# A graph-attention kernel on one core: how the sorted table is turned and decoded between its two edge loops

## What is computed

```
# layer 0
f    = (edge_attr @ fc_w.T).reshape(-1, 4, 128)
feat = sum_over_heads(leaky_relu(attn[edge_type] * f, 0.2))
x    = layernorm(x + segment_sum(x[src] + feat, dst))
# layer 1, on the new x; softmax over the edges of one src
h    = x @ W.T + b;  s1 = h @ a1 + a1b;  s2 = h @ a2 + a2b
e    = leaky_relu(s1[src] + s2[dst], 0.01)
att  = softmax of e over each src
x    = layernorm(x + segment_sum(att * h[dst], src))
```

## Time and profile before

| | |
|---|---|
| median of three runs | 2538.67 us |
| the profiled execution | 2536.95 us, its span 2535.1 us |
| busy share of the span | TensorE 86%, VectorE 91%, ScalarE 77%, GpSimd (POOL) 72% |
| first loop, stage between, second loop | until about 1497 us, 1497 to 1548 us, from 1548 us |

### The profile page before, as it was taken

How to read it: one execution, slowest core, us unless ns; L and a number is a source line. 1 busy time by engine, 2 the same in 40 slices (tenths; PEclk the granted TensorE clock), 3 DMA queues, 4 the chain that set the end, 5 groups by cost and what they waited for, 6 DMA issues and landing times. The chain is left out here.

```text
span 2535.1 us, 49366 instructions
## 1 busy us (share of the span) xinstructions
PE 2173.4 (86%) x12265; PEld 1562.1 (62%) x12266; DVE 2299.6 (91%) x5975; ACT 1950.8 (77%) x5574; POOL 1824.8 (72%) x1746
## 2 busy tenths in 40 slices
PE   6999999999999999999999974766667777777674
PEld 3566666666666666666666654766667666776664
DVE  9999999999999999999999986778887778888886
ACT  5788888888888888888888854777777777776666
POOL 3477777777777777777777745777777777776662
PEclk8999999999999999999999986899998888888886
DMA  4233333333333333333333324444444444443332
GB/s 139 73 101 104 104 106 101 104 103 104 105 106 102 103 103 104 105 106 101 104 102 105 105 58 98 99 100 100 98 101 99 99 100 101 98 99 86 84 82 71
DMA packets 180816, 250.92 MB, mean 99 GB/s; under 512 B 41103, under 2 KB 110172, under 8 KB 180416
## 3 DMA queue, kind: packets, MB, share of 16 engines
q1 hardware_dynamic: 125088, 145.72, 20.2%
q0 software_dynamic: 55456, 102.13, 17.1%
HBM read 238.37 MB, written 9.31 MB: 98 GB/s over the span
## 5 line engine op out<-in xcount | busy, mean ns | idle before, releaser
L627 POOL DMA_INDIRECT room<-in_x,pk x784 | 925.2, 1180 | 262.5 <-issue 252.5
L1010 PE MATMUL FP<-fc_sb,room 128*128 128x512 f32 x1568 | 832.4, 612 | 2.2 <-issue 2.2
L1019 PE MATMUL WP<-at_p,rel_oh 100*128 100x512 f32 x1568 | 804.2, 594 | 0.0
L671 POOL DMA_INDIRECT room<-h_rows,y x666 | 628.9, 944 | 220.5 <-issue 184.9
L754 ACT ACTIVATE w_sb<-WP 128x512 f32<-128x512 f32 x784 | 464.1, 592 | 224.9 <-PE WP L1019 219.5
L1019 PEld LDWEIGHTS WP<-at_p,rel_oh 100*128 100x128 f32 x1568 | 297.9, 190 | 376.4 <-issue 376.4
L1108 PE MATMUL FP<-ident,room 128*128 128x128 f32 x1664 | 278.2, 319 | 277.3 <-DMA room<-h_rows,y 213.9
L1359 DVE TENSOR_TENSOR z<-FP,w_sb 128x1024 f32<-128x1024 f32 x392 | 478.8, 1221 | 1.5 <-ACT w_sb L754 1.0
L1366 DVE SCALAR_TENSOR_TENSOR y<-z 128x2048 f32<-128x2048 f32 x196 | 452.2, 2307 | 0.0
L1108 PEld LDWEIGHTS FP<-ident,room 128*128 128x128 f32 x1664 | 238.0, 220 | 312.9 <-DMA room<-h_rows,y 246.0
L1010 PEld LDWEIGHTS FP<-fc_sb,room 128*128 128x128 f32 x1568 | 266.6, 190 | 43.3 <-issue 2.6
(11 more groups left out here) (280 smaller groups left out, 3475.5 us busy)
## 6 DMA issues: line engine op xcount, KB each, us to landing
room<-in_e SPq DMA_DIRECT2D x196, 256.0 KB
rel_sb<-in_rel_g SPq DMA_DIRECT2D x196, 200.0 KB
z<-sorted_sources SPq DMA_DIRECT2D x208, 128.0 KB
room<-in_x,pk POOLq DMA_INDIRECT x784
room<-h_rows,y POOLq DMA_INDIRECT x666
w_sb<-far_rows SPq DMA_DIRECT2D x100, 65.0 KB
w_sb<-near_records SPq DMA_DIRECT2D x101, 61.0 KB
sorted_edges<-runs,spot_i POOLq DMA_INDIRECT x196, 2.0
```

The costliest lines, as they stand in the source:

```text
L627: pool.indirect_dma_start(xg[:, k, u, 0:P], None, x[:, :], bass.IndirectOffsetOnAxis(ap=pk[:, g, u:u + 1], axis=0)).then_inc(xg_in[k], 16)
L671: pool.indirect_dma_start(hg[k][:, u, :], None, h_dram[:, :], bass.IndirectOffsetOnAxis(ap=sd[:, g * TG + u:g * TG + u + 1], axis=0)).then ...
L1010: mm = pe.matmul(FP[u // 2][:, u % 2, :], e_sb[:, k, u, :], fc_sb[:, :], start=True, stop=True)
L1019: mm = pe.matmul(WP[u % 2][:, :], rel_oh[:, k % 2, u * P:(u + 1) * P], at_p[:, j, :], start=(j == 0), stop=(j == 1))
```

## The change

1. TensorE no longer waits for the sum of the sides. It waits for the table itself and adds the sides in PSUM: for each of the eight tiles two matmuls against the identity, one per side.
2. VectorE's sum, casts and mask of the table leave the pass for chunk 4 and stand behind the last chunk, after the shift L1490.
3. SP's two stores of them stand behind its last store of h.
4. ScalarE's queue stores the last ten rows of the last four blocks, in place of POOL's (the count moves from `h_small` to `h_out`).
5. POOL reads the number of further groups ahead of its h stores, in place of behind them. It waits for `s_loc` ahead of the gathers of group 4, whose buffer is the memory of `tab_sum`.

```diff
@@ sync
-                if c == HCHUNKS // 2:
-                    sp.wait_ge(s_loc, 1)
-                    sp.dma_start(loc_dram..., loc_b...).then_inc(loc_out, 16)
-                    sp.dma_start(near_dram..., loc_i[NEAR_PER * TG - 1:P:NEAR_PER * TG, :]...).then_inc(near_out, 16)
+            sp.wait_ge(s_loc, 1)
+            sp.dma_start(loc_dram..., loc_b...).then_inc(loc_out, 16)
+            sp.dma_start(near_dram..., loc_i[NEAR_PER * TG - 1:P:NEAR_PER * TG, :]...).then_inc(near_out, 16)
             sp.wait_ge(loc_out, 16)
             sp.wait_ge(near_out, 16)
@@ gpsimd
             pool.memset(o_all, 0.0).then_inc(o_zero, 1)
-            for c in range(HCHUNKS):
+            more = group_count(pool)
+            for c in range(HCHUNKS - 1):
                 pool.wait_ge(n_hb, HC * (c + 1))
                 pool.dma_start(h_blocks[PMAIN:BN, HC * c:HC * (c + 1), :],
                                h_sb[PMAIN:BN, HC * c:HC * (c + 1), 0:HROW]).then_inc(h_small, 16)
-            pool.wait_ge(h_out, 16 * HCHUNKS)
-            pool.wait_ge(h_small, 16 * HCHUNKS)
+            pool.wait_ge(h_out, 16 * (HCHUNKS + 1))
+            pool.wait_ge(h_small, 16 * (HCHUNKS - 1))
...
-            more = group_count(pool)
             for k in range(S1):
+                if k == SLOTS:
+                    pool.wait_ge(s_loc, 1)
                 group1(k, k, True)
@@ scalar
-
+            act.wait_ge(n_hb, NS)
+            act.dma_start(h_blocks[PMAIN:BN, NS - HC:NS, :], h_sb[PMAIN:BN, NS - HC:NS, 0:HROW]).then_inc(h_out, 16)
             act.wait_ge(s_dec, 1)
@@ tensor
                 if c == HCHUNKS // 2 - 2:
-                    pe.wait_ge(t_sum, 1)
+                    pe.wait_ge(s_srt, 32)
                     for u in range(CH):
-                        mm = pe.transpose((EPS_T, AP_)[u // 4][:, u % 4 * P:(u % 4 + 1) * P],
-                                          tab_sum[:, u * P:(u + 1) * P], ident[:, :])
+                        for side_of in range(2):
+                            mm = pe.matmul((EPS_T, AP_)[u // 4][:, u % 4 * P:(u % 4 + 1) * P],
+                                           tab[:, side_of, u * P:(u + 1) * P], ident[:, :],
+                                           start=(side_of == 0), stop=(side_of == 1))
                     mm.then_inc(t_turned, 1)
@@ vector
-                if c == HCHUNKS // 2 - 2:
-                    dve.wait_ge(s_srt, 32)
-                    v.tensor_tensor(tab_sum, tab[:, 0, :], tab[:, 1, :], ALU.add).then_inc(t_sum, 1)
-                    dve.wait_ge(t_sum, 1)
-                    link(v.tensor_copy(loc_i, tab_sum))
-                    link(v.tensor_scalar(loc_m, loc_i, 255, P - 1, ALU.bitwise_and, ALU.bitwise_xor))
-                    v.tensor_copy(loc_b, loc_m).then_inc(s_loc, 1)
             dve.wait_ge(t_cast, 1)
             v.tensor_scalar(sd, both, 8, None, ALU.arith_shift_right).then_inc(s_dec, 1)
+            dve.wait_ge(s_srt, 32)
+            v.tensor_tensor(tab_sum, tab[:, 0, :], tab[:, 1, :], ALU.add).then_inc(t_sum, 1)
+            dve.wait_ge(t_sum, 1)
+            link(v.tensor_copy(loc_i, tab_sum))
+            link(v.tensor_scalar(loc_m, loc_i, 255, P - 1, ALU.bitwise_and, ALU.bitwise_xor))
+            v.tensor_copy(loc_b, loc_m).then_inc(s_loc, 1)
             link(v.tensor_scalar(ss, both, 255, P - 1, ALU.bitwise_and, ALU.bitwise_xor))
             dve.wait_ge(s_loc, 1)
             dve.wait_ge(near_out, 16)
             v.tensor_copy(ssf, ss).then_inc(s_ssf, 1)
```

More of the change, by code:

```diff
@@ L544, in _ @@
                              h_sb[0:PMAIN, HC * c:HC * (c + 1), 0:HROW]).then_inc(h_out, 16)
-                if c == HCHUNKS // 2:
-                    sp.wait_ge(s_loc, 1)
[L547 to L550, removed]
+            sp.wait_ge(s_loc, 1)
+            sp.dma_start(loc_dram.rearrange("g (u r) -> (g u) r", r=P).rearrange("(c p) r -> p c r", p=P),
+                         loc_b.rearrange("p (c r) -> p c r", r=P)).then_inc(loc_out, 16)
+            sp.dma_start(near_dram.rearrange("(c a) r -> a c r", c=CH),
+                         loc_i[NEAR_PER * TG - 1:P:NEAR_PER * TG, :].rearrange("p (c r) -> p c r", r=P)).then_inc(near_out, 16)
             sp.wait_ge(loc_out, 16)
@@ L595, in _ @@
             sp.sem_inc(sp_turn, 1)
-            sp.wait_ge(h_out, 16 * HCHUNKS)
-            sp.wait_ge(h_small, 16 * HCHUNKS)
+            sp.wait_ge(h_out, 16 * (HCHUNKS + 1))
+            sp.wait_ge(h_small, 16 * (HCHUNKS - 1))
             for q0, q1 in CHUNKS:
```

## The result

Twenty runs of the changed kernel have a median of 2542.64 us (2540.93 to 2545.30), twenty of the one before 2537.90 us (2536.13 to 2540.43). The ratio is 1.0019, with a 95% interval of 1.0013 to 1.0025: slower by 4.7 us, between 3.3 and 6.3. The forecast was +4.7 us and 2543.4 us, with a hole in the stream of gathers that GpSimd (POOL) issues as its cause.

What follows compares the result with a forecast made beforehand. POOL's gather stream was taken to bound loop 2. VectorE 5.2 us late (+5.9 from L1490 to the cast, less 0.6), less 0.5 of gap, gives +4.7: 2538.67 + 4.7 = 2543.4 us, range 2539.3 to 2546.0.

Steps and rivals of the forecast that it cites:

- The bound: Loop 2: POOL's gathers, about 1.25 us each, have no slack for about 750 us, so any delay moves everything behind.
- Part 1, chunk 5: Pass for chunk 4: TensorE's table matmuls replace VectorE's decode, so chunk 5's statistics begin 0.6 us earlier, not 3.3.
- Part 2, the near store: Behind the last chunk: VectorE's cast into `ssf` waits for the near store, landing 2.6 us after issue; preparation 5.2 us late.
- Part 3, POOL: Start of POOL's stream: first gather some 3.2 us earlier, then 8 us idle for ScalarE's copy; short loop's gather +4.7 us.
- L690 0.3 us after it: POOL's short-loop gather L690 goes 0.3 us, the gap of its stream, after ScalarE's copy L908 ends: at 1556.25.
- a span that grows less than L690 moved: Sign of a wrong forecast: total time grows less than the short loop's gather shifts, meaning unseen slack in loop 2.
- The first gather decides: Rival at POOL's stream start: group 2 follows the first eight gathers, gaining 3.2 us, 2535.5 us; chance 0.08.
- Matmuls at half clock: Rival at TensorE's table matmuls: all run at half clock, 3.8 + 0.6 us more, +9.1, 2547.8 us; chance 0.05.
- The near store lands late: Rival on SP's queue: near store shares the 256 KB store's 3.8 us, 1.2 more; +5.9, 2544.6 us; chance 0.15.
- The delay is taken up later: Rival in loop 2's last 48 steps: consumers are the bound there, loss shrinks to about +1, 2539.7 us; chance 0.12.

Runs made afterwards that it cites:

- two parts and later: Kernel before plus ScalarE's store of the last rows, POOL's early read and the short loop behind group 3's gathers; 2535.67 us beside 2539.16, ratio 0.9987.
- store and read only: Kernel before with only ScalarE's queue storing the last ten rows and POOL reading the group count early; 2537.64 us beside 2538.13, ratio 0.9999.
- own buffer: Changed kernel with the integer sum in other memory, so VectorE's cast to `ssf` skips the near store's wait; 2540.29 us beside 2538.13, ratio 1.0007.
- later, own buffer: Changed kernel with the short loop behind group 3's gathers and the integer sum in its own memory; 2534.02 us beside 2539.16, ratio 0.9979.
- tiles spread: Changed kernel, short loop behind group 3, table matmuls spread over passes for chunks 3 to 10, ScalarE's casts moved to chunk 11; 2531.71 us beside 2539.16, ratio 0.9971.
- short loop later: Changed kernel with POOL running the short loop behind the gathers of group 3, not group 1; 2533.56 us beside 2538.13 before, ratio 0.9979.

## Why the prediction was right, point by point

- **The bound.** That POOL's stream is the bound of loop 2 and passes a shift on is shown: stream shifts of +5.3, -0.2, +0.1, +2.3, -4.7, -2.9, -6.5 and -3.7 us go with medians of +4.7, +0.2, -0.5, +2.2, -4.6, -3.5, -7.4 and -5.1 us, in the order of the table. At the 600th gather of the stage, some 730 us later, the shifts are still +5.5, -0.1, +0.1, +2.7, -4.7, -1.8, -6.6 and -3.8 us; only "two parts and later" lost a microsecond on the way. Behind that, where the last 48 steps have another bound, the shift of the last gather differs from these by up to 1.5 us in single traces.
- **Part 1, chunk 5.** 0.6 us was forecast and 1.1 was measured. The matmuls took 0.11 us each and not 0.125, the rate of loop 2. That it would be far less than 3.3 was right.
- **Part 2, the near store.** Forecast: `s_loc` at 1538.0, cast at 1541.2, 5.2 us late. Measured: the decode ends at 1536.76 + 0.69 = 1537.45, the near store goes at 1537.92, and the cast starts at 1541.01, 5.07 us late. The cast went 3.1 us behind the issue of the near store, not 2.6; the chunks' larger gain made up for that. The other four kernels with the decode behind the chunks have 2.6 to 3.0 us from that issue to what waits for it. The 256 KB store ahead of it landed after 2.7 us in the five kernels that issue it behind the last store of h, and after 3.7 or 3.8 in the four that issue it among them. The Trainium skill, DMA: Bandwidth & Descriptors, section Anatomy of one DMA — SWDGE (gpsimd) path, gives the fit of the prediction (2.0 us plus the bytes over 436 GB/s) for DMAs of GpSimd's queue; these stores go by SP's. Estimated by it, the 256 KB would take 2.6 us, near the 2.7, and both stores would be in at 1537.48 + 2.75 = 1540.2; the cast came 0.8 later, and no run shows why.
- **Part 3, POOL.** The first gather was forecast at about 1538 and came at 1537.13, the hole at 8 us and was 9.14. The step that was mis-sized is "L690 0.3 us after it": I took the gap of a running stream for the distance from a copy to the gather that waits for it. That is 0.80 or 0.81 us in every run in which POOL idled for the copy, and was in the earlier trace rows too, where 1551.56 - 1550.75 = 0.81. I had read this as 0.4 us of POOL's own work and slack; "store and read only" shows that there was none. With 0.81 the forecast for the gather's shift would have been +5.2; it was +5.31, and the time moved by 4.7, between 3.3 and 6.3.
- **Luck in the number.** That the forecast meets the measured +4.7 to the tenth is luck. The chunks gained 0.5 us more than forecast and the near store cost 0.5 more, and these two cancel: the copy came 5.3 us late, where 5.2 was forecast. The gap was 0.5 too short, and the medians moved by 0.6 less than the stream.
- **The signs.** One sign of being wrong was a span that grows less than L690 moved. The medians did (4.7 against 5.3), the spans of the two traces did not (6.8), and the interval holds 5.3; so slack in loop 2 is not shown. One reading had no consequence but was off: `s_loc` had not come 21 us before anyone needed it. It came at 1513.38, and SP's store of `loc_b` used it at 1521.46.
- **The rivals.** "The first gather decides" is excluded by "store and read only" and by the changed kernel's own trace. "Matmuls at half clock" is excluded: the granted clock was 1.00 from 1508.75 to 1514. "The near store lands late" was half true, 0.5 us of its 1.2, and its reason, a share in the 3.8 us, was not: the store ahead landed after 2.7. "The delay is taken up later", with its +1, is excluded by the interval of 3.3 to 6.3 us; that up to 2 of the stream's 5.3 us are taken up later is not.

The 256 KB store after the change, in the list of DMA issues (KB, us to landing):

```profile
sorted_sources<-hs SPq DMA_DIRECT2D x1, 256.0 KB, 2.7
```

The windows that show the clock (stretch, length, busy time of PE, PEld, DVE, ACT, POOL, granted clock, DMA):

```profile
1508.75:1512.25 3.50, 3.50 (x34) 3.50 (x33) 1.59 (x11) 2.58 (x8) 0.55 (x1) 1.00 0.54 136
1512.25:1514.00 1.75, 1.75 (x19) 1.75 (x17) 1.03 (x5) 0.00 (x0) 0.00 (x0) 1.00 0.00 0
```

TensorE stays at its upper level (2.4 GHz, granted clock 1.00) where it had been at the lower one (0.50). Before the change it had paused for the sum ahead of the table's tiles, and that pause is gone:

```profile
1511.25 1.12 PE L1082 MATMUL EP<-ident,room 128*128 128x128 f32 x4 [2.36 <-DVE room L1484]
```

## What to carry to other kernels

Before work is moved off a stage, follow the in-order engine that bounds the next one to its second and third wait, not only to its first. Here the start of the stream came 4 us earlier and its first eight gathers hid a chain that ended 5 us later, so the move turned into a hole. A store whose landing is free in the middle of a loop costs nearly its full latency where its source is overwritten next (3.0 us here). And where an in-order queue waits for a late helper, moving that one instruction a few places back (one number here) can be worth more than making the helper faster: against the change it brought some 9 us, and the 3 us taken off the helper in "own buffer" some 2.5.

## What the runs showed of the hardware that was not expected

GpSimd's gathers take longer to issue beside VectorE's wide copies and casts. In the running stream a gather's record is mostly 0.94 us; in the changed kernel's trace the one at 1541.22, beside the cast L1497 at 1541.01, takes 1.30, and the first, beside L1493 and the mask behind it, 1.24. In "own buffer", where the first gather meets two of them, and in "later, own buffer" it takes 1.55:

```profile
1538.35 0.69 DVE L1493 CAST hs<-w_sb 128x1024 bf16<-128x1024 int32 x1
1538.41 1.55 POOL L671 DMA_INDIRECT room<-h_rows,y  x1 [3.77 <-DMA h_rows<-arena]
```

These are timeline rows of "own buffer". The Trainium skill, SBUF — State Buffer, section SBUF: two separate sides, says that GpSimd is kept from writing descriptors while VectorE runs an operation in a two-port mode. The traces agree in that the longer records, 0.1 to 0.6 us more per gather, stand beside such casts; which mode these ran in no trace shows. From the first gather to the stream "tiles spread" takes 22.37 us and "later, own buffer" 22.29, against 21.56 in "short loop later". All of these 0.8 and 0.7 us lie in longer records. That VectorE's port is the reason is likely and not shown; no run took the casts away to show it alone. The same rule bears on the ten rows: POOL's last store before the change took 1.02 us to issue and the slowest landed after 4.9; with ScalarE's queue the first gather came 2.7 us earlier, part of which is the register read, and the two were not told apart.
